# First convolution on 32x32 array tiles straight from the map buffer, GpSimd power in four normalisations

## The reference, cut to what matters

```python
x = x + _L0_conv_ref(_gn(x), W1, W2, bias_w)   # Volterra 3x3: 9 linear taps and 45 products of two taps
x = x + _L1_conv_ref(_gn(x), weight, bias)     # a 3x3 convolution
x = x + _L2_conv_ref(_gn(x), ...)              # attention: 1024 queries, 900 keys, 4 heads of 8, per image
x = x + _L3_conv_ref(_gn(x), weights1)         # Hartley transform, mixing of modes, transform back
def _gn(v):  # per image and channel
    return (v - mean(v)) / sqrt(var(v) + 1e-5)
```

## Time and profile before

| what | value |
|---|---|
| median of 3 runs | 377.89 us (376.87 to 380.81) |
| the profiled execution's own time | 378.51 us |
| its span in the profile | 376.5 us |
| busy: TensorE, VectorE, ScalarE, GpSimd | 317.9, 230.0, 173.3, 38.9 us |
| stage 1, from `xp` to the transpose L761 | 8.15 to 66.35 us |
| stage 2 and the convolutions of the attention | 66.4 to 116.9 us |
| attention | 116.9 to 320.4 us |
| last stage | 320.4 to 376.5 us |

### The profile page before, as it was taken

The page is one execution under the profiler, slowest core; times in us unless marked ns, Lnnn a source line. Parts: engine busy times, 40 slices in busy tenths (PEclk is TensorE's granted clock), DMA queues, the critical chain, the costliest instruction groups (busy, mean ns, idle before and its releaser), DMA issues.

```text
span 376.5 us, 5797 instructions
## 1 busy us (share of the span) xinstructions
PE 317.9 (84%) x2186; PEld 109.5 (29%) x2186; DVE 230.0 (61%) x494; ACT 173.3 (46%) x334; POOL 38.9 (10%) x36
## 2 busy tenths in 40 slices
PE   5499655688998553999999999999999899885994
PEld 1133111232343111323332323323333222332931
DVE  5970054744836650468778687878776321579944
ACT  2100000002416443987879787897978787300000
POOL 5000600400000000001010000101010012505100
PEclk9989968999989865999999999999999999999798
DMA  2799995000157953230210303000000000000001
GB/s 85 163 196 211 190 200 162 0 3 0 38 166 147 124 109 125 84 113 2 60 55 1 113 3 113 2 1 3 0 1 2 1 3 0 2 0 1 3 2 56
DMA packets 6867, 23.89 MB, mean 63 GB/s; under 512 B 1272, under 2 KB 2040, under 8 KB 5912
## 3 DMA queue, kind: packets, MB, share of 16 engines
q1 hardware_dynamic: 6840, 23.53, 26.0%
HBM read 11.59 MB, written 2.37 MB: 37 GB/s over the span
## 4 chain that ended last, share of the span: by engine, by line
PE 48%; DVE 9%; issue 4%; ACT 2%; DVEq 0%; ACTq 0%
PE ps L1179 14%; PE ps L1161 14%; PE ps L1138 11%; DVE arena_a L463 3%; PE ps L1291 2%; ACT arena_b L678 2%; PE ps L1184 2%; PE ps L1234 1%; PE ps L1251 1%; DVE arena_a L966 1%; PE ps L1007 1%; PE ps L1299 1%; DVE arena_b L978 1%; DVE arena_a L990 1%; PE ps L1242 1%
## 5 line engine op out<-in xcount | busy, mean ns | idle before, releaser
L678 ACT ACTIVATE arena_b<-ps 128x512 f32<-128x512 f32 x232 | 125.2, 607 | 37.6 <-PE ps L1161 36.9
L1161 PE MATMUL ps<-arena_a 128*128 128x512 bf16 x224 | 85.0, 389 | 10.1 <-issue 9.5
L1138 PE MATMUL ps<-arena_a 128*128 128x450 bf16 x256 | 87.4, 371 | 6.5 <-issue 4.3
L890 DVE TENSOR_REDUCE mx<-ps 128x1 f32<-128x450 f32 x120 | 69.3, 618 | 6.5 <-PE ps L1138 4.8
L885 DVE CUSTOM_DVE_ANT_0 sums<-ps,relus 128x450 bf16<-128x450 f32 x68 | 41.4, 626 | 44.3 <-PE ps L1138 34.9
L1179 PE MATMUL ps<-arena_b,vt 128*32 128x512 f32 x448 | 59.7, 605 | 0.7 <-ACT arena_b L678 0.7
L1161 PEld LDWEIGHTS ps<-arena_a 128*128 128x128 bf16 x224 | 21.7, 98 | 80.6 <-ACT arena_b L678 50.4
L686 ACT ACTIVATE relus<-ps 128x450 f32<-128x450 f32 x68 | 37.5, 554 | 10.5 <-PE ps L1138 10.4
L1007 PE MATMUL ps<-zeros 128*128 128x512 bf16 x115 | 30.4, 406 | 7.7 <-DMA xa<-x 3.5
L1138 PEld LDWEIGHTS ps<-arena_a 128*128 128x128 bf16 x256 | 24.0, 100 | 39.9 <-issue 11.3
L640 ACT ACTIVATE arena_b<-ps 96x386 f32<-96x386 f32 x3 | 1.5, 490 | 63.9 <-PE ps L1056 63.8
(11 more groups left out here) (130 smaller groups left out, 244.2 us busy)
## 6 DMA issues: line engine op xcount, KB each, us to landing
arena_b<-arena_a SPq DMA_DIRECT2D x12, 578.0 KB, 10.3
arena_b<-wmodes SPq DMA_DIRECT2D x4, 1024.0 KB, 4.9
arena_a<-k_scratch SPq DMA_DIRECT2D x3, 516.8 KB
arena_b<-arena_a SPq DMA_DIRECT2D x4, 306.0 KB, 5.7
arena_a<-q_scratch SPq DMA_DIRECT2D x3, 384.0 KB
arena_b<-arena_a SPq DMA_DIRECT2D x4, 272.0 KB, 5.0
k_scratch<-arena_b SPq DMA_DIRECT2D x3, 344.5 KB, 3.7
cst<-consts SPq DMA_DIRECT2D x1, 1029.0 KB, 11.7
```

Source lines behind the costliest of these rows:

```text
L678: nc.scalar.activation(probs[:, n % PRING, :], ps[:, SCORE_RING[n % len(SCORE_RING)], :], ACT.Exp).then_inc(expd, 1)
L890: nc.vector.tensor_reduce(mx[:, a, e:e + 1], bank, AX.X, ALU.max).then_inc(max_read, 1)
L1138: mm(ps[:, block_bank(i), 0:KHALF], qst[:, e, g, qt * P:(qt + 1) * P], kst[:, g, at:at + KHALF], start=True, stop=True).then_inc(max_score ...
L1161: last = mm(ps[:, bank, :], kst[:, g, t * P:(t + 1) * P], qst[:, e, g, :], start=True, stop=True)
```

## The change

Stage 1: `stack` and its 20 DMAs go, as do the shifted double maps. VectorE makes 12 maps (13 with ScalarE's square, 14 with x), all in two cuts, the upper 612 elements of every map first, then the lower 544. TensorE reads `maps` itself with tiles of 32 rows x 32 columns: image b gives the row group, the position j of a pair in its round of four gives the column group, and the result of (b, j) lands on partitions 32j of bank 2b+e. So 54 pairs are 14 rounds (the last with two), of 16 matmuls each, for each half. Each bank then holds four partial sums under each other: ScalarE and VectorE copy two banks each per half to `l0q`, and four matmuls with `jsum` (four identities under each other) add them up and put them where the old result was. The weights of the stage grow from 544 to 1728 columns; SyncE loads the other constants right behind them.

Normalisation, all four: the integer guess and two of three Newton steps are replaced by a power -0.5 on GpSimd (`rsqrt`), with a semaphore there and one back. GpSimd's list has these at four places, the first behind the fills at the start.

Fills: `qst` and `kst` are no longer filled with zeros and ones; the matmuls read 72 or 75 rows, and the three rows of ones come by a DMA (`ones_in`) from a row that GpSimd fills. `xst` is zeroed right after the first normalisation (`padded`, 1), not after the stage. The fillers at the start: 6 of the old form, 3 of 225 columns in float32r, 8 of 32 rows of that kind, 8 of 32 rows in bfloat16; before it was 12, then 20 in four groups tied to the maps.

```diff
-TILES = [...]
+MAPS = [LINEAR, (0, 0), (0, 1), (1, 0), (1, 1), (1, -1), (2, 0), (0, 2), (1, 2), (1, -2), (2, 1), (2, -1), (2, 2), (2, -2)]
+PAIRS = [(m, py, px) for m, d in enumerate(MAPS) for py in range(3) for px in range(3) if tap_pair(d, py, px)]
+ROUNDS = [PAIRS[i:i + COL_TILES] for i in range(0, len(PAIRS), COL_TILES)]
 # SyncE
-            for cut, signal in enumerate((tile0_top, tile_in[0])):
-                sp.wait_ge(act_map, 2 * cut + 2)
-                sp.wait_ge(map_ready, 2 * cut + 2)
-                stack_tile(0, *CUTS[cut], signal)
-            for t in range(1, len(TILES)):
-                sp.wait_ge(map_ready, SLOTS_PER_TILE * (t + 1))
-                if t == 3:
-                    sp.wait_ge(tile0_used, 1)
-                stack_tile(t, 0, NP, tile_in[t])
             sp.dma_start(cst[:, N_FIRST:N_CONST], consts[:, N_FIRST:N_CONST]).then_inc(consts_loaded, 16)
+            sp.wait_ge(l0_half, 2)
+            sp.wait_ge(ones_set, 1)
+            sp.dma_start(kst[PAIR_ROWS:S_ROWS, :, 0:KEYS],
+                         ones_row.unsqueeze(1).to_broadcast([PARTS, G, KEYS])).then_inc(ones_in, 16)
 # GpSimd
+            nc.gpsimd.memset(minus_half[:], -0.5).then_inc(zeros_ready, 1)
+            pool.wait_ge(zeros_ready, 2)
+            nc.gpsimd.tensor_copy(zeros_r[:], zeros[:, 0:KHALF]).then_inc(zeros_ready, 1)
             nc.gpsimd.memset(xp[:], 0.0).then_inc(xp_zeroed, 1)
 ...
+            def rsqrt(n):
+                pool.wait_ge(var_ready, n + 1)
+                nc.gpsimd.tensor_tensor(small[:, 3:4], small[:, 2:3], minus_half[:], ALU.pow).then_inc(rsqrt_done, 1)
+                pool.wait_ge(rsqrt_done, n + 1)
+            rsqrt(0)
+            nc.gpsimd.memset(ones_row, 1.0).then_inc(ones_set, 1)
+            pool.wait_ge(padded, 1)
+            nc.gpsimd.memset(xst[:], 0.0).then_inc(xst_zeroed, 1)
-            nc.gpsimd.memset(arena_a[64:P, 0:q_words], 0.0).then_inc(q_filled, 1)
 # VectorE, normalisation
-                link(nc.vector.tensor_scalar(v, var, EPS, None, ALU.add))
-                link(nc.vector.tensor_scalar(y.bitcast(I32), v.bitcast(I32), -0.5, float(0x5F3759DF),
-                                             ALU.mult, ALU.add))
-                for _ in range(3):
-                    link(nc.vector.scalar_tensor_tensor(t, y, nh, y, ALU.mult, ALU.mult))
-                    link(nc.vector.scalar_tensor_tensor(y, t, 1.5, y, ALU.add, ALU.mult))
+                nc.vector.tensor_scalar(v, var, EPS, None, ALU.add).then_inc(var_ready, 1)
+                norms[0] += 1
+                dve.wait_ge(rsqrt_done, norms[0])
+                dve.wait_ge(dve_step, chain[0])
+                link(nc.vector.scalar_tensor_tensor(t, y, nh, y, ALU.mult, ALU.mult))
+                link(nc.vector.scalar_tensor_tensor(y, t, 1.5, y, ALU.add, ALU.mult))
 # VectorE, evacuation (ScalarE has the same for b in (0, 2))
+            for e in range(2):
+                dve.wait_ge(l0_half, e + 1)
+                for b in (1, 3):
+                    nc.vector.tensor_copy(l0q[:, b, e * HALF:(e + 1) * HALF], ps[:, 2 * b + e, :]
+                                          ).then_inc(l0_evac_dve, 1)
+            dve.wait_ge(l0_summed, 2)
-                nc.vector.memset(arena_a[64:P, w0:w1], TWO_ONES).then_inc(k_filled, 1)
 # TensorE
             for e in range(2):
+                needed = 0
+                for i, taps in enumerate(ROUNDS):
+                    if i == 0:
+                        pe.wait_ge(act_map, 2 * e + 2)
+                    newest = max(m for m, _, _ in taps)
+                    if newest > max(needed, 1):
+                        needed = newest
+                        pe.wait_ge(map_ready, e * (N_MAPS - 2) + newest - 1)
                     for b in range(B):
+                        r = slice(32 * b, 32 * b + 32)
+                        for j, (m, py, px) in enumerate(taps):
+                            last = mm(ps[32 * j:32 * j + 32, 2 * b + e, :].rearrange("p (y x) -> p y x", x=W),
+                                      l0w[r, COL_TILES * i + j, :], window(maps[r, m, :], py, px, 16 * e, 16, W),
+                                      start=(i == 0), stop=(COL_TILES * (i + 1) + j >= len(PAIRS)), skip_group_check=True)
+                last.then_inc(l0_half, 1)
             pe.wait_ge(consts_loaded, 16)
+            for e in range(2):
+                pe.wait_ge(l0_evac_act, 2 * e + 2)
+                pe.wait_ge(l0_evac_dve, 2 * e + 2)
+                for b in range(B):
+                    last = mm(ps[32 * b:32 * b + 32, e, :], c_("jsum"), l0q[:, b, e * HALF:(e + 1) * HALF],
+                              start=True, stop=True)
+                last.then_inc(l0_summed, 1)
 # attention
-                mm(ps[:, block_bank(i), 0:KHALF], qst[:, e, g, qt * P:(qt + 1) * P], kst[:, g, at:at + KHALF],
+                mm(ps[:, block_bank(i), 0:KHALF], qst[0:PAIR_ROWS, e, g, qt * P:(qt + 1) * P],
+                   kst[0:PAIR_ROWS, g, at:at + KHALF],
```

More of the change, by code:

```diff
@@ L40 @@
 I32 = mybir.dt.int32
+F32R = mybir.dt.float32r
 ACT = mybir.ActivationFunctionType
@@ L329, in build @@
         map_ready = sem("map_ready")
-        tile0_top = sem("tile0_top")
-        tile_in = [sem(f"tile_in{t}") for t in range(len(TILES))]
-        l0_done = sem("l0_done")
+        l0_evac_act = sem("l0_evac_act")
+        l0_evac_dve = sem("l0_evac_dve")
+        l0_half = sem("l0_half")
+        l0_summed = sem("l0_summed")
+        ones_set = sem("ones_set")
+        ones_in = sem("ones_in")
         l0_read = sem("l0_read")
@@ L591, in _ @@
             pool.wait_ge(k_zeroed, 2)
+            rsqrt(2)
             pool.wait_ge(xin_act, 2)
@@ L618, in _ @@
             nc.gpsimd.memset(arena_a[:, 0:8192], 0.0).then_inc(xm_zeroed, 1)
+            rsqrt(3)
             pool.wait_ge(tu_ready, 8)
@@ L741, in _ @@
             dve.wait_ge(padded, 1)
[L742 to L753, removed]
[L754 to L758 removed]
+            for n0, n1 in CUTS:
+                for m, (dy, dx) in list(enumerate(MAPS))[2:]:
+                    at = dy * WP + dx
+                    nc.vector.scalar_tensor_tensor(maps[:, m, n0:n1], xp[:, n0:n1], VOLTERRA_SCALE,
+                                                   xp[:, at + n0:at + n1], ALU.mult, ALU.mult).then_inc(map_ready, 1)
+            for e in range(2):
[4 more added lines that the diff above has]
+            dve.wait_ge(l0_summed, 2)
             dve.wait_ge(first_loaded, 16)
[L760 removed]
             nc.vector.transpose(l0t.rearrange("p (j o) -> p j o", o=32),
@@ L1018, in _ @@
             for e in range(2):
-                rows = [slice(32 * b, 32 * b + 32) for b in range(B)]
-                for s, (t, (py, px)) in enumerate(SLOTS):
-                    if t == 0:
-                        if s == 0:
-                            pe.wait_ge(tile_in[0] if e else tile0_top, B * 16)
-                        for b in range(B):
-                            last = mm(ps[rows[b], e, :].rearrange("p (y x) -> p y x", x=W), l0w[:, s, :],
-                               window(stack[:, 0, b, :], py, px, 16 * e, 16, W), start=(s == 0), stop=False,
-                               skip_group_check=True)
@@ L1028, in _ @@
-            last.then_inc(tile0_used, 1)
-            for s, (t, (py, px)) in enumerate(SLOTS):
-                if t == 0:
-                    continue
-                if SLOTS[s - 1][0] != t:
-                    pe.wait_ge(tile_in[t], B * 16)
-                for e in range(2):
-                    for b in range(B):
-                        last = mm(ps[32 * b:32 * b + 32, e, :].rearrange("p (y x) -> p y x", x=W), l0w[:, s, :],
-                                  window(stack[:, t % 3, b, :], py, px, 16 * e, 16, W), start=False,
-                                  stop=(s == len(SLOTS) - 1), skip_group_check=True)
@@ L1160, in score_tile @@
                     g = b * HEADS + h
-                    last = mm(ps[:, bank, :], kst[:, g, t * P:(t + 1) * P], qst[:, e, g, :],
+                    last = mm(ps[:, bank, :], kst[0:S_ROWS, g, t * P:(t + 1) * P], qst[0:S_ROWS, e, g, :],
                               start=True, stop=True)
@@ L1165, in score_tile @@
                         g = b * HEADS + h
-                        last = mm(ps[32 * h:32 * h + 32, bank, :], kst[:, g, DT * P:KPAD],
-                                  qst[:, e, g, :], start=True, stop=True)
+                        last = mm(ps[32 * h:32 * h + 32, bank, :], kst[0:S_ROWS, g, DT * P:KPAD],
+                                  qst[0:S_ROWS, e, g, :], start=True, stop=True)
                 last.then_inc(scored, 1)
```

97 lines of the change are left out of this document (45 added, 52 removed), and 4 rows, old and new, of the table TILES.

## The result

The changed kernel takes 354.44 us (median of 4 runs, 348.61 to 355.60), the kernel before beside it 378.07 us. The ratio is 0.928, with a 95% interval of 0.914 to 0.942. Six further runs on another chip gave a median of 353.9 us and a ratio of 0.941 (0.936 to 0.946). The forecast was 348.0 us, 345 to 356.

What follows compares the result with a forecast made beforehand. Stage 1 was taken to be bound by the restacking copies, with what it gains coming off the total. Span 376.5 - 28.5 (stage 1) - 2.0 (normalisations) = 346.0 us, plus 2.0 around it: 348.0 us, range 345 to 356.

Steps and rivals of the forecast that it cites:

- The bound, and the copies: Stage 1, 8.15 to 66.35 us, is bound by the restacking copies; what it gains, 28.5 us, comes off the total.
- Start of TensorE: First round of stage 1 may start at 9.55 us (up to 11), after ScalarE's upper cuts and the weights.
- The matmuls: Stage 1's 28 rounds, 864 records: 24.8 us (23.9 by columns, up to 31.2 by records), plus 0.8 for the clock.
- The tail: End of stage 1, from last matmul to transpose: PSUM copies, four adding matmuls and handoffs, 2.7 us; transpose at 37.85 us.
- The normalisations: With a power of 0.3 us on GpSimd, normalisations 2, 3 and 4 gain 0.67 us each, 2.0 in all; the first nothing.
- Reading 75 rows in place of 128 leaves the number of columns, and so the time, as it is.: Attention's matmuls reading fewer rows: costed at nothing.
- The rest: Fills, second constants, SyncE's list and GpSimd's fills behind the waits of `rsqrt`: costed at nothing.
- The sum: Whole kernel: 376.5 - 28.5 - 2.0 = 346.0 us of span, plus 2.0 around it, 348.0 us.
- C: GpSimd's first use for other than a fill costs a load of 1.3 to 5.8 us: 349 to 354 us; chance 0.20.
- B's milder form: Stage 1 records start at 36.1 ns, tiles still overlapping: matmuls 31.2 us, total 354.4 us; most of B's 0.11.
- B: Stage 1 rounds slower but tiles overlapping: 354.4 us, or 371.1 us if row groups overlap two at a time; chance 0.11.
- D: Stage 1 row groups served one after another: matmuls 95.8 us, total 419 us, 11% slower than before; chance 0.07.

Runs made afterwards that it cites:

- three tiles: Changed kernel with the fourth matmul of each image left out in all stage 1 rounds but the first of each half; stage 1 matmuls 24.9 us.
- the supply alone: Changed kernel with 256 columns in place of 512 in all stage 1 rounds but the first of each half; matmuls 24.75 us, 64 every 3.73 us.

## Why the prediction was right, and where not

**The bound, and the copies.** Right: without the copies TensorE is full in stage 1, and this carries the whole gain.

**Start of TensorE.** 9.55 us forecast, 10.02 us found; 0.2 us of it is the later start of the first write, another 0.16 us its greater length. The weights were no limit, they landed at 8.5 us.

**The matmuls.** The term of 24.8 us plus 0.8 for a cold start was mis-sized: 28.6 us at full clock. Neither bound was wrong by itself. Columns alone gave 24.9 us (three tiles) and the supply alone 58 ns a matmul, 25 us, close to the 57 ns that the row of L1275 had given. I took the larger of two bounds that come out nearly equal; together they cost 3.4 to 3.8 us on top of either. How exactly they add up wasn't settled. The 0.8 us for the clock weren't needed: it was 1.00 over all 28.6 us.

**The tail.** 2.7 us forecast, 2.6 us found (38.62 to 41.21).

**The normalisations.** A power takes 0.55 us, not 0.3, so each of the last three gains 0.38 us in place of 0.67; 0.9 us too much in the sum. The first lost 0.25 us by the power, inside the bounds given.

**"Reading 75 rows in place of 128 leaves the number of columns, and so the time, as it is."** This is the step that failed. The columns did stay, but the granted clock came back later behind the rest at the entry. It cost 1.4% in the old kernel (3.7 us between the medians), and 4.3 us between the medians of the changed one (353.9 against 349.6 us, the fills moved to GpSimd included). I had asked what the fills cost and not what the filled rows did.

**The rest.** The fills, the loads and the queues behind the new waits cost nothing that shows, but one: the fill of the ones' row (7.13 to 7.97 us) ran beside the first write of xp, which took 0.97 us in place of 0.81.

**The sum.** The profile was 7.3 us over 348.0. Stage 1 is 41.21 us in place of 37.85 (3.4 us), the attention lost 7.3 us, 4.4 by the low clock at its beginning and 2.9 by the second fall of the clock, and an entry 3.4 us shorter, which wasn't forecast either, came back. The 0.9 us of the powers don't show in it: the three stages with such a power were 1.9 us shorter together, nearly the 2.0 forecast, though the powers themselves gave only 1.1. The median was 6.4 us over. That it still lies within 345 to 356 us is luck in part: the range had no room set aside for the attention, and reached to 356 only because it took in C and B's milder form with a cold start.

**Rivals.** B in its form "records slower, tiles still overlapping" is what happened in stage 1, by some 60% of its 6.4 us; that the median, 354.44 us, is all but B's 354.4 is chance, since a good part of the excess comes from the attention. C didn't happen: GpSimd's first copy (at 1.36 us) took 0.56 us, and the first power 0.55 us, as long as the later ones. The page "GPSIMD Engine Reference" of the Trainium skill (2.1) gives about 6 us for a first call of a freshly loaded kernel; this trace shows no such time at these operations. D didn't happen: sixteen tiles overlap, or the matmuls would have taken 96 us.

## What to carry to other kernels

Rows that multiply zeros can matter for TensorE's clock: before cutting them, look whether the stretch begins after a rest at half clock, and compare the granted clock over the same instructions, not the column counts. When two bounds of an engine come out nearly equal (here 24.9 and 25.2 us), don't forecast the larger one alone; here the two together took 28.6 us, 15% more. A stretch measured from one matmul to another needs both in the trace: count the records, and where some are missing go by the weight loads. Before a fill is moved to GpSimd, look what VectorE does beside it.

## What the runs showed of the hardware

- TensorE with fewer rows gets its clock back later. After the rest the mean granted clock over 15 us was 0.54 to 0.74 with 72 and 75 rows (eight profiles), 0.80 to 0.83 with 128 (three), and 1.00 with 128 rows and fillers until 1.9 and 3.6 us before the first matmul (two).
- A fill of GpSimd held up VectorE's TENSOR_SCALAR from SBUF to SBUF in float32: 9.40 us in place of 0.81, ending 0.5 us after the fill of 9.28 us. The products of two inputs (L745) beside the fill of `xst` (3.73 us) went on as usual: the six that ran beside it took 0.78 to 0.80 us each, the six of the same size behind it 0.78 to 0.79. The page "GPSIMD Engine Reference" of the Trainium skill (1) names contention both with VectorE's two-port modes and with two inputs from SBUF; the second isn't seen here, beside a fill, which has no input itself.
- Short matmuls of 32x32 tiles came in groups of 64 every 3.73 us (once 4.00), when the columns didn't hold them back, in step with 16 KB packets of the instruction queue.
